# Moving the PSUM copies of two transposed tiles from VectorE to ScalarE in a Nyström attention and ternary feed-forward layer

## What is computed

```python
xn = layernorm(x)                       # over features
k, q, v = heads(xn @ Wk), heads(xn @ Wq) / 8, heads(xn @ Wv)
q_l, k_l = mean of q, k over each 32 tokens          # 64 landmarks
s1 = softmax(q @ k_l.T)                 # 2048 x 64 per head
s2 = softmax(q_l @ k_l.T)               # 64 x 64
s3 = softmax(q_l @ k.T)                 # 64 x 2048
attn = s1 @ (pinv6(s2) @ (s3 @ v))      # pinv6: six Newton-like iterations
ffn = bit_linear(silu(conv3(bit_linear(xn, w1))), w2)  # 8-bit rows, ternary weights
out = x + attn @ Wo + bo + ffn
```

## Time and profile before

| | us |
|---|---|
| median of the runs (2 runs) | 4264.96 |
| lowest, highest | 4263.6, 4266.33 |
| the profiled execution, its own time | 4260.4 |
| its span (first to last instruction, slowest core, core 6) | 4258.8 |
| spans of the eight cores | 4229.5 to 4258.8 |
| mean granted TensorE clock of the cores | 0.796 to 0.806 of full |

### The profile page before, as it was taken

How to read it: one execution, slowest core, us unless ns; L and a number is a source line. 1 busy time by engine, 2 the same in 40 slices (tenths; PEclk the granted TensorE clock), 3 DMA queues, 4 the chain that set the end, 5 groups by cost and what they waited for, 6 DMA issues and landing times.

```text
span 4258.8 us, 46668 instructions; the slowest of 8 cores (4229.5 to 4258.8 us)
## 1 busy us (share of the span) xinstructions
PE 2139.4 (50%) x11922; PEld 1180.6 (28%) x12052; DVE 1957.1 (46%) x3501; ACT 1310.4 (31%) x2061; POOL 12.8 (0%) x132
## 2 busy tenths in 40 slices
PE   0110226877424556575655118867325547565654
PEld 0000113546412212222212114547312212222212
DVE  2224543123243284848484433123342475757573
ACT  4541222320021062525251453310121243434241
POOL 0000000000000000000000000000000000000000
PEclk9999988985556799898988558975557889898988
DMA  5435682100101303030303221100102202131303
GB/s 140 131 121 188 212 259 71 39 18 1 42 1 42 97 1 107 35 107 35 107 35 97 83 71 51 44 7 1 42 1 75 65 28 99 42 100 40 101 32 106
DMA packets 212931, 305.82 MB, mean 72 GB/s; under 512 B 109596, under 2 KB 126142, under 8 KB 210376
## 3 DMA queue, kind: packets, MB, share of 16 engines
q1 hardware_dynamic: 73544, 197.94, 14.0%
q10 hardware_dynamic: 139136, 104.88, 8.4%
HBM read 244.02 MB, written 58.76 MB: 71 GB/s over the span
## 4 chain that ended last, share of the span: by engine, by line
PE 29%; DVE 26%; DMA 19%; issue 15%; ACT 8%; DVEq 1%; ACTq 1%; SPq 0%; POOL 0%; POOLq 0%
DMA mix<-w2t_sp 8%; PE pb L1522 7%; PE pb L1012 5%; PE pb L775 5%; DVE scr L1413 4%; DVE scr L1365 4%; PE pb L804 3%; DMA h<-w 2%; PE pb L1231 2%; DMA h<-wo_sp 2%; DVE scr L1440 1%; DMA h<-q_sp 1%; PE pb L470 1%; PE pb L1357 1%; DVE mix L1554 1%
## 5 line engine op out<-in xcount | busy, mean ns | idle before, releaser
L1357 PE MATMUL pb<-mix,w1t 128*128 128x512 bf16 x2006 | 528.6, 412 | 301.8 <-DVE scr L1365 274.4
L1522 PE MATMUL pb<-mix,h 128*128 128x512 bf16 x2006 | 502.6, 397 | 253.1 <-DMA mix<-w2t_sp 181.0
L1357 PEld LDWEIGHTS pb<-mix,w1t 128*128 128x128 bf16 x2048 | 198.4, 103 | 632.2 <-issue 472.1
L1400 ACT ACTIVATE scr<-scr,sml 128x512 f32<-128x512 f32 x256 | 208.1, 813 | 501.7 <-DVE scr L1394 299.4
L1522 PEld LDWEIGHTS pb<-mix,h 128*128 128x128 bf16 x2048 | 205.0, 100 | 548.5 <-issue 389.1
L1509 ACT CAST h<-scr 128x512 bf16<-128x512 int16 x256 | 147.1, 615 | 562.5 <-PE pb L1522 439.6
L775 PE MATMUL pb<-mix,h 128*128 128x512 bf16 x1006 | 242.2, 399 | 52.9 <-ACT h L785 29.5
L1506 DVE TENSOR_SCALAR scr<-scr 128x512 int16<-128x512 f32 x256 | 109.3, 427 | 323.7 <-ACT h L1509 301.7
L1012 PE MATMUL pb<-h 128*128 128x64 f32 x960 | 213.7, 422 | 49.4 <-DVE h L1037 22.4
L1012 PEld LDWEIGHTS pb<-h 128*128 128x128 f32 x960 | 207.6, 331 | 60.8 <-issue 60.8
L1424 ACT ACTIVATE h<-scr 128x512 f32<-128x512 f32 x256 | 161.3, 630 | 188.0 <-DVE scr L1419 187.9
(11 more groups left out here) (204 smaller groups left out, 2866.6 us busy)
## 6 DMA issues: line engine op xcount, KB each, us to landing
h<-w SPq DMA_DIRECT2D x64, 512.0 KB
h<-w SPq DMA_DIRECT2D x16, 2048.0 KB
mix<-w2t_sp SPq DMA_DIRECT2D x128, 256.0 KB
mix<-w2t_sp ACTq DMA_DIRECT2D x128, 256.0 KB
h<-wo_sp ACTq DMA_DIRECT2D x64, 256.0 KB
h<-x SPq DMA_DIRECT2D x32, 512.0 KB
out<-mix SPq DMA_DIRECT2D x32, 512.0 KB
scr<-x SPq DMA_DIRECT2D x16, 512.0 KB
```

The lines of the kernel that those rows point to most:

```text
L1357: nc.tensor.matmul(psm.ap[:, 0:TT], self.w1t.ap[:, kc * DH + hc * 128: kc * DH + hc * 128 + 128], xq_b.ap[:, kc * TT:(kc + 1) * TT], start ...
L1400: nc.scalar.activation(acc1.ap[:, 0:TT], hcur.ap[:, 1:TT + 1], AF.Identity, bias=self.cb.ap[:, hc:hc + 1], scale=self.cw2.ap[:, 3 * hc + 1 ...
L1522: ps_o=ps_o, wb=wb: nc.tensor.matmul(ps_o.ap, h2q[:, hc * 1024 + tb * 128: hc * 1024 + tb * 128 + 128], wb.ap[:, half * 512:half * 512 + 512],
```

## The change

In `tail` of B1 and in the block loop of B3 the copies from PSUM of transposed tiles are recorded for ScalarE (`nc.scalar.copy`) in place of VectorE (`nc.vector.tensor_copy`). The shapes, the buffers and the place in the text stay as they are.

```diff
@@ phase_B1, tail
                 self.op("pe", emits, reads=[p3, self.idb_sb], writes=[psb])
-                self.op("dve", lambda g=g, gn=gn, pbf=pbf:
-                        nc.vector.tensor_copy(
+                self.op("act", lambda g=g, gn=gn, pbf=pbf:
+                        nc.scalar.copy(
                             p3t.ap[:, g * 1024:g * 1024 + gn * 128],
                             pbf[:, 0:gn * 128]),
                         reads=[psb], writes=[p3t])
@@ phase_B3, block loop
-            self.op("dve", lambda par=par, pbf=pbf: nc.vector.tensor_copy(
+            self.op("act", lambda par=par, pbf=pbf: nc.scalar.copy(
                 s1t[par].ap[:, 0:512], pbf[:, 0:512]),
                 reads=[pstr], writes=[s1t[par]])
...
-            self.op("dve", lambda par=par, pbf=pbf: nc.vector.tensor_copy(
+            self.op("act", lambda par=par, pbf=pbf: nc.scalar.copy(
                 s1t[par].ap[:, 512:1024], pbf[:, 0:512]),
                 reads=[pstr], writes=[s1t[par]])
```

## The result

| | us |
|---|---|
| before, median | 4264.8 |
| changed, median | 4278.5 |
| ratio of the two, 95% interval | 1.0039 (1.0023 to 1.0054) |
| forecast | 4283 (1.0043) |
| spans of the eight cores, changed, profiled execution | 4240.8 to 4274.6 |

A forecast was written before the change was run, and what follows sets the result against it. The prediction took serial chains in B3 and B1's tails, with the copies as links, to be the bound. Terms of 10.1 and 8.3 us gave 18.4 on 4260.4; with the median 4.6 higher, it forecast 4283 us, range 4268 to 4300.

The forecast's parts named there:

- The price of a copy: Moved PSUM copies in B1 and B3: 583 ns on ScalarE against 424.5 for 128x512, 1005 against 692 for 128x1024.
- B3: Term for B3: 64 copies, each 158.5 ns longer with no cover, hand-offs unchanged; 10.1 us.
- the bound of 3.2 us for longer hand-offs: B3: if ScalarE's hand-off to TensorE always cost 0.25 us, 32 of them add 0.1 each.
- B1: Term for B1's 16 tails: 13 x 0.49 + 2 x 0.80 + 0.31 = 8.3 us.
- The usual tail: B1, 13 of 16 tails: L741 starts 0.49 us later, at 766.74 against 766.25.
- tails with early transposes: B1, pairs 1 and 6 of the first sequence: moved copies queue behind ScalarE's last lam3 copy, +0.80 us each.
- The last tail of a sequence: B1: counted among the 13 tails of the usual shape, +0.49 us.
- Long hand-offs: Rival: long hand-offs and long copies, every bound at its upper end; +35 us, 4300 us; chance 0.08.
- Table loads: Rival: B1 and B3 alternate exponential and copy, 96 function table loads of 1.283 us; +123 us, 4388; chance 0.02.
- Relief of VectorE: Rival: if VectorE were the bound, its 49 us of moved copies would come off; 4216 us; chance 0.01.
- ScalarE as the better engine for PSUM: Rival: bf16 copies follow the f32 rows, 583 against 692 ns; 64 copies win 7 us, 4258; chance 0.02.
- The clock: Rival: the clock shifts for the worse; 18 + 10 us, 4293 us; chance 0.06.

The follow-up runs named there:

- two single-part kernels: The move made in one stage only, B3 alone or B1 alone; ratios to the kernel before 1.0011 and 1.0004.
- two-bank kernels: B3's second transposes get their own PSUM bank; copies on VectorE, on ScalarE (B1 moved too), or one on each: ratios to before 0.9929, 0.9987, 0.9942.
- b3only: The changed kernel with B1's copies put back on VectorE, so only B3's are moved; ratio to the kernel before 1.0011.
- b2_f32_act: The kernel before with B2's transposed f32 PSUM copies (L1034, 24 in all) moved to ScalarE; ratio to before 1.0001.
- halves_both: The kernel before with two banks in B3, copies on VectorE and ScalarE, halves of s1t tracked apart; block 11.05 us.
- waits_ahead: The changed kernel with two already met waits ahead of VectorE's at B1's exponential; negation to exponential 0.25 us, B1 287.9 / 287.1 us.
- two_banks_both: The kernel before with two banks in B3, first copy on VectorE, second on ScalarE; ratio to before 0.9942.

## Why the prediction was right

**What bounds the kernel.** The reading that both copies are links of a serial chain, that VectorE's free time is worth nothing there, and that nothing else waits in ScalarE's queue held in both stages. The two single-part kernels show it stage by stage, and the two-bank kernels show it from the other side: the same copies with one of them beside TensorE's work are worth 29 us. The mechanism was right, and so was the sign. The size came out less well than the whole time suggests: by stage the two terms, forecast as 10.1 and 8.3 us, measured 8.2 and 6.4, so 14.6 in place of 18.4. That the ratio, 16.6 us, lies nearer to the forecast is chance, as 1.2 us of it are in other stages and its interval is 13 us wide.

**The price of a copy.** 583 and 1005 ns were forecast from a line through ScalarE's rows for other widths and types; 586 and 1013 were measured. That a copy from bf16 is no shorter on ScalarE, and is on VectorE, is what decided the sign.

**B3.** Forecast 0.317 us a block and 10.1 us in all. Measured: 0.27 to 0.28 in the usual block, so 8.2 us by stage in the changed kernel and 8.7 in `b3only`. The term that was too large is the hand-off, which I had taken as equal on both engines. The first copy's transposes before the change are this row:

```profile
1301.71 0.59 PE L1175 MATMUL pb<-idb_sb,scr 128*128 128x128 bf16 x4 [5.52 <-DVE scr L1166]
```

VectorE started its copy at 1302.40, 0.69 us later, and ScalarE 0.67 us after its transposes (1302.16 - 1301.49). As the median over all blocks and cores it is 0.68 instead of 0.69, and after the second transposes 0.73 instead of 0.76. The way back costs 0.25 to 0.26 us after the first copy and 0.14 to 0.15 after the second, on either engine. So the bound of 3.2 us for longer hand-offs had the wrong sign. The remainder is in single blocks: before, some took 0.1 to 0.4 us longer than the usual 11.91, at the same places in every core, and with the change these sit elsewhere. What causes them is open.

**B1.** Forecast 8.3 us. From transposes to L741 the 16 tails took 45.7 us in all in core 6 before and 54.1 in core 1 after, and as the mean of eight cores 45.2 and 53.6, +8.4 either way: the term was right in sum, but that is luck, as two of its parts were off in opposite directions. The usual tail has its +0.49.

In core 6 the tails with early transposes were those of pairs 1 and 7, where the prediction has 1 and 6, and in part that of pair 5. They are early because TensorE had the higher clock: there the 16 transposes took 1.05 us at a granted clock of 1.00 (2.4 GHz), in the usual tails 1.91 us at 0.50 (1.2 GHz). So which step a tail pays depends on the clock of the moment: on the eight cores 22 of 128 tails were early before and 35 with the change.

For an early tail I had let the first copy queue behind the end of the last `lam3` copy; the timeline of such a pair shows that it starts 0.1 us before that end, so the distance is 3.05 us instead of 2.35 and the step 0.70 instead of 0.80. The last two lines are the windows of L725 in this pair and in the usual pair shown above (us, busy by engine, granted clock):

```profile
834.17 2.61 ACT L866 COPY scr<-pb 128x512 f32<-128x512 f32 x4
...
835.88 1.05 PE L725 MATMUL pb<-idb_sb,h 128*128 128x128 bf16 x16
836.67 2.12 ACT L734 COPY h<-pb 128x1024 bf16<-128x1024 bf16 x2
...
838.93 1.05 PE L741 MATMUL pb<-h 128*128 128x128 bf16 x16 [2.00 <-ACT h L734]
...
835.88:836.93 1.05, 1.05 (x17) 0.88 (x15) 0.00 (x0) 0.96 (x3) 0.00 (x0) 1.00 0.00 0
766.11:768.02 1.91, 1.91 (x17) 1.64 (x15) 0.00 (x0) 1.45 (x3) 0.00 (x0) 0.50 0.00 0
```

The last tail of a sequence grew by 0.75 instead of 0.49. There L741 has four waits on three semaphores where it had two on two before, and starts 0.46 us after the copies' end instead of 0.25:

```profile
951.16 2.11 ACT L734 COPY h<-pb 128x1024 bf16<-128x1024 bf16 x2 [1.41 <-PE pb L725]
...
953.73 1.86 PE L741 MATMUL pb<-h 128*128 128x128 bf16 x16 [1.87 <-ACT h L734]
```

What the sum left out is the exponential: 14 pairs win back 0.11 us each, 1.5 us, as the moved copies take its waits. 8.4 - 1.5 = 6.9, against 6.4 by stage (6.0 over the executions named above). I had read the list of waits in the order of instructions before and after, where it stood, and priced only the copies.

**The rivals.** Long hand-offs: no, they were shorter by 0.01 to 0.03 us. Table loads: the changed kernel has the same four loads as before, none in B1 or B3. Relief of VectorE: no. ScalarE as the better engine for PSUM: true for f32 (B2), false for bf16. The clock: B1's lengths moved with the waits and copies, and the mean granted clock of the cores was 0.794 to 0.807 where it had been 0.796 to 0.806, so within the resolution of this kernel it gave nothing and took nothing; no run here holds the clock fixed, so a share of it in the microsecond or two between sum and stage is not excluded.

## What to carry to other kernels

Price a copy by its rows for the same type, width and memory on the engine that is to take it; where only other widths stand, two of them give a line and a third checks it. In a serial stage the choice of engine is worth the difference of two durations, some tenths of a microsecond for each copy, while a second bank or a finer-tracked buffer takes the whole copy off the chain: 8 us lost by the first in B3, 46 us won by the second there. And when an instruction moves, read the waits of its new neighbours as well as its own: those behind the one that decides cost time, those ahead don't.

## What the runs showed of the hardware

A wait that is already met cost nothing ahead of the deciding one and 0.055 us behind it, on ScalarE (L874 to the exponential: 0.25 us with none behind, 0.36 with two). VectorE's L1188, with one behind, started 0.76 us after its transposes' start where L1179, with none, started 0.69. On TensorE a wait behind cost about 0.105 us, and this accounts for several distances that the prediction and the sections above took singly (the deciding wait is the one whose releaser came last):

| waits behind the deciding one | TensorE's instruction | starts after the releaser's end, us |
|---|---|---|
| 0 | L741, first L1194 | 0.14 to 0.15 |
| 1 | L1184; L741 in the last tail, before | 0.25 to 0.26 |
| 2 | L1012 in `b2_f32_act` | 0.37 |
| 3 | L741 in the last tail, changed | 0.46 |

In three of the kernels here two neighbouring cores took 8 to 24 us longer in B1 alone, at a lower granted clock, with no difference in the program that would explain it. Windows over 680 to 960 us of `halves_both`, cores 2 and 4 (busy time by engine, then granted clock, DMA share, GB/s):

```profile
680.00:960.00 280.00, 243.79 (x1884) 147.96 (x1881) 52.85 (x115) 88.88 (x155) 0.00 (x0) 0.76 0.10 33
680.00:960.00 280.00, 222.48 (x1961) 138.62 (x1960) 63.91 (x130) 93.33 (x160) 0.00 (x0) 0.89 0.11 36
```

Core 2's B1 took 305.0 us, core 4's 282.2; the clock was 0.76 against 0.89. Core 3 had it with core 2, and in the second sequence cores 0 and 1. Cores 0 and 1 of `waits_ahead` (both sequences) and of `two_banks_both` (the first) had it too. What sets it off is open. It is one reason for reading a step of 5 us from stages and rows here, not from whole times.
